# Placing the value mixing beside P.V in a hand-ordered two-layer macaron kernel

## The reference, cut to what matters

```python
q = einsum('btc,hdc->bhtd', x, Wq);  k = einsum('btc,hdc->bhtd', x, Wk)      # 16 heads of 64
w, sel = top_k(einsum('btc,hec->bthe', x, Ws), 2)                            # 8 experts, top 2
mix_v = einsum('bthk,bthke->bthe', sigmoid(w), one_hot(sel, 8))
proj_v = einsum('btc,edc->bted', x, Wv)
v = einsum('bthe,bted->bhtd', mix_v, proj_v)                                 # value mixing
attn = einsum('bhij,bhjd->bihd', softmax(q * scale @ k), v)                  # scores, P.V
_, sel_o = top_k(einsum('btc,hec->bthe', x, Wd), 2)                          # second top 2
res = einsum('bthe,bthd,efd->bthf', one_hot(sel_o).sum(3), attn, Wo).sum(2)  # output product
```

## Time and profile before

| | |
|---|---|
| median of 3 runs | 2648.18 us (2647.19 to 2648.7) |
| the profiled execution | 2646.63 us, span of its instructions 2644.8 us |
| PE busy | 2476.0 us, 94% of the span |
| DVE busy | 2101.0 us, 79% |
| ACT busy | 1914.7 us, 72% |
| mean granted TensorE clock | 0.984 of full |
| PE waiting for the first of DVE's takes of `back` ahead of `out` (L844 for L1114) | 21.1 us in 10 places |

### The profile page before, as it was taken

One profiled execution on the slowest core, in us unless ns is written; L12 is line 12 of the kernel. 1 busy time (PEld: TensorE's weight loads), 2 busy tenths in 40 slices (PEclk: granted clock), 3 DMA queues, 4 the chain that ended last, 5 costly groups with the idle time before them and its releaser, 6 DMA issues.

```text
span 2644.8 us, 50256 instructions
## 1 busy us (share of the span) xinstructions
PE 2476.0 (94%) x16925; PEld 1576.0 (60%) x16925; DVE 2101.0 (79%) x3154; ACT 1914.7 (72%) x4558; POOL 738.6 (28%) x564
## 2 busy tenths in 40 slices
PE   5599999999999899999889999999999999999998
PEld 3355665655656556565565656656565656666665
DVE  7588786989879789888986998789788878866553
ACT  3366767877788578867776877788687878877674
POOL 1000001452145126504440453155035315500000
PEclk9799999999999999999999999999999999999999
DMA  3413334553455435455444553455455345544424
GB/s 142 123 42 79 92 89 124 158 137 97 99 153 162 98 107 132 140 133 131 117 104 121 155 135 104 117 154 144 113 157 159 100 110 153 143 107 112 104 69 96
DMA packets 636714, 318.58 MB, mean 120 GB/s; under 512 B 419568, under 2 KB 545584, under 8 KB 636080
## 3 DMA queue, kind: packets, MB, share of 16 engines
q1 hardware_dynamic: 630416, 313.54, 45.2%
q10 hardware_dynamic: 6048, 1.84, 0.3%
HBM read 241.36 MB, written 82.31 MB: 122 GB/s over the span
## 4 chain that ended last, share of the span: by engine, by line
PE 56%; DVE 24%; issue 10%; POOL 3%; DMA 3%; ACT 2%; SPq 1%; ACTq 0%; DVEq 0%; POOLq 0%
PE ps L755 12%; PE ps L764 11%; PE ps L777 10%; DVE h_ring L1281 7%; PE ps L744 6%; PE ps L823 4%; DVE h_nmax L1102 4%; PE ps L838 3%; PE ps L844 2%; POOL h_ring L691 2%; DVE h_ring L1291 2%; DMA h_pv<-pv_d 1%; PE ps L796 1%; PE ps L829 1%; POOL h_wide_c L700 1%
## 5 line engine op out<-in xcount | busy, mean ns | idle before, releaser
L943 ACT ACTIVATE h_prob<-ps,h_nmax 128x512 f32<-128x512 f32 x1024 | 715.0, 700 | 106.4 <-DVE h_nmax L1102 104.8
L1102 DVE TENSOR_REDUCE h_nmax<-ps 128x2 f32<-128x1024 f32 x512 | 621.5, 1214 | 126.3 <-PE ps L755 124.8
L764 PE MATMUL ps<-ident,h_prob 128*128 128x128 f32 x4096 | 619.8, 277 | 23.5 <-ACT h_probT L1067 14.2
L764 PEld LDWEIGHTS ps<-ident,h_prob 128*128 128x128 f32 x4096 | 472.2, 141 | 190.0 <-issue 109.3
L755 PE MATMUL ps<-h_qk 64*128 64x512 f32 x2048 | 579.9, 643 | 0.1
L1067 ACT ACTIVATE h_probT<-ps 128x512 f32<-128x512 f32 x796 | 482.6, 606 | 93.7 <-PE ps L764 90.7
L700 POOL TENSOR_TENSOR h_wide_c<-h_wide_c,h_ring 128x512 f32<-128x512 f32 x240 | 332.4, 1385 | 647.6 <-DVE h_ring L1291 647.5
L777 PE MATMUL ps<-h_probT,h_v_sb 128*64 128x256 f32 x4096 | 499.9, 386 | 5.6 <-ACT h_vT L995 2.4
L777 PEld LDWEIGHTS ps<-h_probT,h_v_sb 128*64 128x64 f32 x4096 | 272.1, 137 | 311.3 <-issue 147.1
L1281 DVE TENSOR_TENSOR_SCAN h_ring<-h_ring 128x512 f32<-128x512 f32 x256 | 399.5, 1561 | 34.2 <-POOL h_ring L691 17.9
L691 POOL TENSOR_TENSOR h_ring<-h_m_xpad,h_m_b_rows 128x512 f32<-128x512 f32 x256 | 351.5, 1383 | 238.6 <-DVE h_m_xpad L1402 230.0
(11 more groups left out here) (224 smaller groups left out, 2715.7 us busy)
## 6 DMA issues: line engine op xcount, KB each, us to landing
h_mix_diag<-mix_blocks SPq DMA_DIRECT2D x128, 512.0 KB, 4.2
at_d<-h_att SPq DMA_DIRECT2D x128, 256.0 KB, 2.4
h_m_b_rows<-dbl_d SPq DMA_DIRECT2D x128, 256.0 KB, 4.3
h_m_c_rows<-dbl_d SPq DMA_DIRECT2D x128, 256.0 KB, 4.2
h_mo_diag<-mo_blocks SPq DMA_DIRECT2D x120, 256.0 KB, 3.3
h_att<-at_d SPq DMA_DIRECT2D x120, 256.0 KB, 3.7
pv_d<-h_pv SPq DMA_DIRECT2D x64, 256.0 KB, 2.9
h_pv<-pv_d SPq DMA_DIRECT2D x256, 64.0 KB, 3.4
```

Of the source, the lines that this page charges most:

```text
L764: ins = pe.transpose(ps[:, TB + v % 2, k * P:(k + 1) * P], prob[:, v % NB, k * P:(k + 1) * P], ident[:, :])
L943: act.activation(prob[:, v % NB, :], ps[:, SB + v % 4, :], ACT.Exp, bias=nmax[:, p, j, o:o + 1], accum_out=den[:, p, j, o:o + 1]).then_inc ...
L1102: dve.tensor_reduce(nmax[:, p, j, :], ps[:, SB + 2 * w % 4:SB + 2 * w % 4 + 2, :], X, ALU.max, negate=True).then_inc(sem("row_max"), 1)
```

## The change

Only step numbers and one order change; no operation is added or taken away.

- The heads of job 0 start 46 steps behind the start of its preparation, not 51.
- Of the value mixing, chunks 1 and 2 stand in step 58, 3 and 4 in step 62, 5 and 6 in step 2 of the next job (66), 7 in step 6 (70), each behind the P.V of that step; chunk 0 stands in step 55. Before, they were at 56, 57, 58, 61, 63, 0, 2 and 3. `vmix` now sorts with rank 0, behind `att` by its name.
- The values are transposed (`vturn`) at 8 and 9 instead of 4 and 8, and at 54 instead of 55.
- The output product goes from step 50 to 51, the second top-2 from steps 44 to 55 to steps 48 to 59.
- Smaller ones: `value` 3 from 31 to 30, `f_z` 0 from 15 to 18, `f_turn` 0 from 37 to 36.

```diff
         FIRST_PREP = 57
-        START = FIRST_PREP + 51
+        START = FIRST_PREP + 46
...
             "heads": [(4 * a + 10, "att", a) for a in range(HALF)] + [(8 * p + 17, "back", p) for p in range(PAIRS)]
-            + [((4, 8, 15, 23, 31, 39, 47, 55)[p], "vturn", p) for p in range(PAIRS)] + [(8 * p - 5, "pq", p) for p in range(PAIRS)] + [(8 * p - 4, "pk", p) for p in range(PAIRS)],
-            "post": [((18, 22, 26, 30, 32, 38, 42, 46)[c], "omix", c) for c in range(NCO)] + [(50, "out", 0)],
+            + [((8, 9, 15, 23, 31, 39, 47, 54)[p], "vturn", p) for p in range(PAIRS)] + [(8 * p - 5, "pq", p) for p in range(PAIRS)] + [(8 * p - 4, "pk", p) for p in range(PAIRS)],
+            "post": [((18, 22, 26, 30, 32, 38, 42, 46)[c], "omix", c) for c in range(NCO)] + [(51, "out", 0)],
...
-            + [((21, 23, 26, 31)[j], "value", j) for j in range(J)]
-            + [((56, 57, 58, 61, 63, 64, 66, 67)[c], "vmix", c) for c in range(NCV)],
-            "first_prep": [((46, 47, 48, 49, 50, 51, 52, 53)[c], "vmix", c) for c in range(NCV)],
-            "front": [(15, "f_z", 0), (19, "f_lin", 0), (27, "f_norm", 0), (28, "f_key", 0), (32, "f_val", 0)]
-            + [((29, 31, 33, 35)[j], "f_score", j) for j in range(J)] + [((37, 38, 39, 44)[j], "f_turn", j) for j in range(J)]
+            + [((21, 23, 26, 30)[j], "value", j) for j in range(J)]
+            + [((55, 58, 58, 62, 62, 66, 66, 70)[c], "vmix", c) for c in range(NCV)],
+            "first_prep": [((47, 48, 49, 50, 51, 52, 53, 54)[c], "vmix", c) for c in range(NCV)],
+            "front": [(18, "f_z", 0), (19, "f_lin", 0), (27, "f_norm", 0), (28, "f_key", 0), (32, "f_val", 0)]
+            + [((29, 31, 33, 35)[j], "f_score", j) for j in range(J)] + [((36, 38, 39, 44)[j], "f_turn", j) for j in range(J)]
...
-        FIRST_IN_STEP = {"att": 0, "omix": 1, "vmix": 1}
+        FIRST_IN_STEP = {"vmix": 0, "att": 0, "omix": 1}
...
-        TOP_AT = (AT["gate", 1] + 3, 44)
+        TOP_AT = (AT["gate", 1] + 3, 48)
```

## The result

| | before | after |
|---|---|---|
| median on one chip, four runs each | 2648.05 us (2647.19 to 2648.7) | 2617.09 us (2614.27 to 2621.05) |
| ratio to before | | 0.9884 [0.9867, 0.9901] |
| profiled execution, span | 2646.63, 2644.8 us | 2621.05, 2619.3 us |

The change saves 31 us, 1.2%. The forecast was 2602 us, faster, with a range of 2586 to 2632: the direction and the range held, and the gain was 15 us smaller than the 46 us of the sum. The profiled execution is the slowest of the four, so sizes are read from medians of runs wherever an experiment gives one.

The account below looks back on a forecast made before the run. TensorE, busy 94% of the span, was taken to set the time. The terms -17 - 27 + 8 - 6 + 3 - 7 = -46 us took 2646.6 to 2600.6; with 1.6 for the median, 2602 us, range 2586 to 2632.

Parts of the forecast that it names:

- 1, mixing beside P.V, -17: Value mixing on PE: pieces paired and behind P.V save 1.11 us a job over 15 jobs, 17 us.
- 2, output product and top-2, -27 + 8: Steps 48 to 51: output product waits less for DVE, 27 us gained; later top-2 operations cost 8 us.
- the 8 that the prediction set: Sign of being right: the output product's wait (L844) for DVE's take (L1114) under 8 us in sum.
- the +8: Steps 56 to 59: four top-2 operations a job just fit on DVE; cost between 0 and 20 us, 8 taken.
- Rival A: DVE's lateness only moves from step 50 to step 58; 2621 us, chance 0.24.
- the 15 that was to decide for it: Sign against the forecast: the mixing's wait (L823) for DVE's take (L1114) over 15 us.
- 3, loads, -6: Chunk loads for value mixing: pairs four steps apart hide nearly all landing time, saving 6 of 11.7 us waited.
- the sign named, under 5: Sign of being right: the mixing's waits (L823) for DMA loads under 5 us.
- Rival D: At steps 62 and 2 the pairs wait for their second chunk, making the kernel slower; 2656 us, chance 0.07.
- 4, values turned at 8 and 9, +3: First P.V at step 10 needs DVE's take sooner; between -2 and +8 us, 3 us cost taken.
- 5, START 46, -7: Lead-in: heads of job 0 start earlier, first P.V at 132 instead of 139.4; gain 0 to 12 us, 7 taken.
- 6, 0: Smaller moves of f_z, f_turn 0, value 3 and vturn 7 into gaps: no gain, 0 +- 2 us.

Follow-up runs that it names:

- x3: Changed kernel with the value mixing of jobs 1 to 15 at its old steps and old rank: 2622.48 us, ratio 0.9915.
- x8: Changed kernel with the chunks behind P.V moved one step on, a transpose group between: 2644.26 us, ratio 0.9997.
- x12: Changed kernel with the load of x issued at step 2 instead of 5, ahead of chunk 7's load: 2605.93 us, ratio 0.985.
- x1: Kernel before with two edits alone, output product at step 51 and second top-2 at steps 48 to 59: 2626.12 us, ratio 0.9925.
- x4: Changed kernel with the second top-2 back at steps 44 to 55, output product still at 51: 2624.24 us, ratio 0.9916.
- x2: Changed kernel with the heads of job 0 starting at step 51 of its preparation again: 2623.64 us, ratio 0.9917.
- x7: Changed kernel with the first transposes of the front layers (`f_z` 0) at step 15 again: 2615.94 us, ratio 0.9885.
- x10: Changed kernel with the value mixing in pairs at 55, 62, 66 and 70, none in step 58: 2623.77 us, ratio 0.9912.
- x6: Changed kernel with the heads transposed one step earlier, except pair 7: 2625.01 us, ratio 0.9916.

## Why the prediction was right, and where its sum was off

**1, mixing beside P.V, -17.** The size is right: 17 us less least time (x3 against after), and 18 us come back when the groups stand alone (x8). In after only 8 us of it reach the time; with the load of x early 17 us do (x12 against x3).

The Trainium skill (TensorEngine Tiling (Array Packing), Tiling Modes, Key Properties) says that a change of tiling mode drains TensorE; the prediction's estimate from it was 15 us, with ten changes fewer a job. By the prediction's own count of places there are ten before and two after, so eight fewer, and 12 us. The traces agree that such a group costs time, some 0.3 us for going in and coming out together; that a drain is the reason isn't shown, since x8 changes the neighbours and the shape at once.

**2, output product and top-2, -27 + 8.** Right: -20 us by themselves (x1), -25.5 us in the stretch of steps 48 to 51, L844's wait 6.1 us, below the 8 that the prediction set. What was wrong is the +8: with the old mixing the top-2 operations add 1 us of waiting in steps 56 to 59 (16 to 17), with the new mixing 11 (x4's 8 to after's 19). Rival A's mechanism is therefore real but partial, 11.6 us and under the 15 that was to decide for it. The price of one such wait is more than its length. Step 58 of job 2 of after, timeline of PE:

```profile
567.14 1.95 PE L777 MATMUL ps<-h_probT,h_v_sb 128*64 128x256 f32 x16
572.13 3.68 PE L823 MATMUL ps<-h_mix_diag,h_pv 128*64 128x256 f32 x16 [3.04 <-DVE h_att L1114]
```

DVE's take began at 571.38, 6.45 us after PE's transposes at 564.93. After 3.04 us of idleness the pair takes 3.68 us instead of 1.90: 1.8 us on top of the 3.0. The granted clock of 572.1 to 575.8 us is 0.50, the half level, and 0.79 over steps 56 to 59 of that job.

**3, loads, -6.** The wait of L823 for loads is 5.6 us instead of 11.7, as forecast; the sign named, under 5, was just missed, but 5.4 of the 5.6 stand in the lead-in, and in the steady part it went from 5.3 us to 0.2. The second load of a pair does land later, as the prediction estimated (1.5 us more): 5.75 us from issue to landing in the median, where the first of a pair takes 4.2 and a single one 4.1. Issued 1.75 us behind the first it lands 7.5 us after the first's issue in the median, inside the 8.2 us that PE leaves; the longest, 7.8 us from its own issue, would not be. Rival D didn't happen.

**4, values turned at 8 and 9, +3.** In after too small: before P.V at step 10 PE now waits 8.4 us and before the turn 4.1, while the norm transpose gave up 4.7 (7.7 to 3.0): +8, the end of the range named. But the order of the turns isn't the cause. In x12, with that order and the load early, the same three places come to about 3.4, 4.3 and 0 us, together the 7.7 of before. **The step that failed** is in part 3: there the loads moved on SP were followed only to the rows of the Mamba scan behind them, and only as issue time. Step 3 has not six issues but three (chunk 7's); what counts is that they wait for step 2. The load of x stands in the same queue, issued 5 us later against PE, and DVE's norm, row maxima and take of back 7 hang on it. x12 takes that one cause away, and 9 us come back.

**5, START 46, -7.** Right: x2 gives 8.7. After's own trace shows none of it (first P.V at 139.12, before 139.41), because its lead-in is the latest of the ten traces with START 46: they run from 129.0 to 139.1 us, 134.5 in the mean. The four with START 51 run from 139.4 to 145.2, 142.5 in the mean, 8 us later. In after the chain of eight chunks took 28.2 us (104.6 to 132.8) against 24.1 in before; the first P.V followed 6.3 us behind, not the 12.8 of before. One trace is no measure of a lead-in that varies by 10 us.

**6, 0.** Right (x7).

Together: -46 was the forecast and -31 came. Some 9 us are SP's queue (x12). The other 6 are open. Some 3 of them fit the top-2 operations in steps 56 to 59, 11 us of waiting where the sum had 8; the rest is within what these differences can tell. Neither is isolated, since x10, which clears step 58, makes SP's queue worse at the same time. That the forecast's range held although a whole chain of waits was missing from the sum is partly luck: the range was set by term 2's bounds, not by this chain. The terms alone don't add up either: 19.9 (x1) + 8.7 (x2) + 8.2 (x3) = 36.8, where the whole gives 31, the last two good to some 6 us each. A version with both x12's load and another place for chunk 1 wasn't tried.

## What to carry to other kernels

Work that moves on one engine must be followed through every in-order queue that serves it: here a load that waits for its buffer held back an unrelated load behind it, and PE felt it through DVE three links later. If a wait for a late engine is removed by moving the piece that waits, look at the next piece that needs the same engine (x6). What ended lateness here was moving the late engine's own work into a stretch where it had time (x1, 20 us, with the output product a step later) or getting its input earlier (x12, 9 us). Grouping matmuls of the same tile shape took 17 us out of PE's list, but half of that was lost until the wait that came with the new order was found.

## What the runs showed of the hardware

Matmul groups of 64-column tiles cost some 0.3 us each for standing by themselves between transposes: 18.3 us over the 56 places of jobs 1 to 14 in which x8 and after differ; prices taken from a few rows of before (0.30 us a place) gave the same within 2 us in total. Behind a wait of 3.04 us the next 16 records ran at the half clock level (granted clock 0.50), 3.68 us instead of 1.90. Of two chunk loads of 640 KB in flight, issued some 1.75 us apart, the second lands 1.6 us later than a single one in the median (its `mix_diag` part, 5.75 against 4.1 us from issue, 46 pairs in after), the first hardly later (4.2).
